# Experts of a decoder: results scattered by the names of their tokens and read back with plain loads

## The reference

```
scores = sigmoid(xt @ gate.T)
_, sel = top_k(scores + expert_bias, TOP_K)
order = argsort(sel.reshape(-1), stable=True)
token_idx = order // TOP_K;  expert_ids = sel.reshape(-1)[order]
xb = (xt[token_idx] * scores_sorted[:, None]).astype(bfloat16)
for e in range(8):
    h = silu(xb @ w1e.T) * (xb @ w3e.T)
    out_r += where(expert_ids == e, h @ w2e.T, 0)
out = (silu(xt @ shared_w1.T) * (xt @ shared_w3.T)) @ shared_w2.T
out = out.at[token_idx].add(out_r)
x = layernorm(x + out)
```

## Time and profile before

| | |
|---|---|
| median of 3 runs | 2945.8 us (2944.82 to 2948.53) |
| the profiled execution: its own time | 2947.47 us |
| its span, first to last instruction | 2945.7 us |
| mean granted TensorE clock | 0.958 |
| busy: PE, DVE, ACT, POOL | 2639.9, 1988.5, 1464.4, 1199.9 us |
| the stage `experts` begins at | about 2674 us |
| its first block begins on PE at | 2796.17 us |
| its last block's result stands in `ex_oe` at | 2871.6 us |
| its last output tile is made at | 2935.9 us |

### The profile page before, as it was taken

How to read it: one execution, slowest core, us unless ns; L and a number is a source line. 1 busy time by engine, 2 the same in 40 slices (tenths; PEclk the granted TensorE clock), 3 DMA queues, 4 the chain that set the end, 5 groups by cost and what they waited for, 6 DMA issues and landing times. The chain is left out here.

```text
span 2945.7 us, 47353 instructions
## 1 busy us (share of the span) xinstructions
PE 2639.9 (90%) x16941; PEld 1760.8 (60%) x16941; DVE 1988.5 (68%) x2542; ACT 1464.4 (50%) x2868; POOL 1199.9 (41%) x1106
## 2 busy tenths in 40 slices
PE   8999899888888888886999899999997889997886
PEld 5666645534444444443999777777775555556653
DVE  4788757689999999966112079999999733333353
ACT  3444413289999998862222166666666311112410
POOL 0000025446666565542222058688888500001304
PEclk9999999989999999997999999999999999997898
DMA  2123513269888887964002221011112271111163
GB/s 97 65 77 116 201 51 100 77 133 168 170 170 163 170 172 162 191 154 159 32 29 74 100 79 45 26 55 58 51 51 94 77 129 36 43 66 58 61 151 118
DMA packets 534873, 296.52 MB, mean 101 GB/s; under 512 B 438160, under 2 KB 482192, under 8 KB 530832
## 3 DMA queue, kind: packets, MB, share of 16 engines
q1 hardware_dynamic: 518720, 260.31, 35.1%
q0 software_dynamic: 15952, 33.56, 4.0%
HBM read 126.43 MB, written 62.78 MB: 64 GB/s over the span
## 5 line engine op out<-in xcount | busy, mean ns | idle before, releaser
L1181 DVE TENSOR_REDUCE xh_top<-xh_seen 128x1 f32<-128x512 f32 (+1 forms) x768 | 631.3, 863 | 46.0 <-PE xh_seen L1083 32.5
L1153 ACT ACTIVATE xh_prob<-xh_sc,xh_bias,xh_scale 128x1024 int16<-128x1024 f32 (+1 forms) x512 | 609.8, 1201 | 69.5 <-PE xh_sc L1083 69.3
L2328 POOL TENSOR_TENSOR ss_state<-ss_du,ss_b_all 128x1024 f32<-128x1024 f32 x128 | 445.7, 3495 | 169.4 <-PE ss_turned L1926 97.8
L1083 PE MATMUL xh_seen<-xh_kT,xh_qT 96*128 96x512 bf16 x1024 | 354.0, 387 | 81.8 <-DVE xh_top L1181 79.8
L2376 DVE TENSOR_TENSOR_SCAN ss_state<-ss_decay,ss_state 128x1024 f32<-128x1024 f32 x128 | 387.3, 3027 | 27.3 <-ACT ss_decay L2178 27.3
L1083 PE MATMUL xh_sc<-xh_kT,xh_qT 96*128 96x512 bf16 x1024 | 309.0, 384 | 1.3 <-ACT xh_prob L1153 1.3
L1207 POOL CAST xh_probT<-xh_pairs 128x2048 int16<-128x2048 uint8 x128 | 241.8, 1889 | 11.3 <-DMA xh_pairs<-xh_prob 2.7
L1083 PEld LDWEIGHTS xh_seen<-xh_kT,xh_qT 96*128 96x128 bf16 x1024 | 89.3, 97 | 242.8 <-DVE xh_top L1181 220.4
L1933 PE MATMUL ss_bank<-ss_xc,hold_w_conv 128*128 128x256 f32 x1024 | 229.3, 379 | 0.7 <-ACT ss_xc L2190 0.7
L2178 ACT ACTIVATE ss_decay<-ss_delta,ss_a 128x255 f32<-128x255 f32 x512 | 210.7, 496 | 0.4
L1933 PEld LDWEIGHTS ss_bank<-ss_xc,hold_w_conv 128*128 128x128 f32 x1024 | 190.0, 189 | 26.4 <-ACT ss_xc L2190 1.1
(11 more groups left out here) (392 smaller groups left out, 4886.5 us busy)
## 6 DMA issues: line engine op xcount, KB each, us to landing
ex_rows_in<-sa_zeros POOLq DMA_DIRECT2D x18, 1024.0 KB, 6.7
ss_b_all<-ss_states SPq DMA_DIRECT2D x8, 2048.0 KB, 7.2
xa_kT<-xp_kT SPq DMA_DIRECT2D x8, 768.0 KB, 5.3
xh_qT<-xa_qT SPq DMA_DIRECT2D x48, 128.0 KB, 3.2
xh_kT<-xa_kT SPq DMA_DIRECT2D x48, 128.0 KB, 3.3
ex_rows_out<-ex_oe SPq DMA_DIRECT2D x23, 256.0 KB, 2.2
sa_x<-in_x SPq DMA_DIRECT2D x8, 512.0 KB, 3.6
sa_y<-in_x SPq DMA_DIRECT2D x8, 512.0 KB, 10.9
```

Of the source, the lines that this page charges most:

```text
L1083: ins = pe.matmul(out[:, c * D:(c + 1) * D], qT[s][:, t * P:(t + 1) * P], kT[s][:, at + c * D:at + (c + 1) * D], start=True, stop=True)
L1153: act.activation(out, scores, ACT.Exp, bias=bias[t % RING][:, :], scale=scale[s][:, t:t + 1], accum_out=total[s][:, half, t:t + 1]).then_i ...
L1181: ins = v.tensor_reduce(top[t % RING][:, k:k + 1], scores[:, 0:n], AX.X, ALU.max)\
L2328: g.tensor_tensor(state[k % RING][:, :, :], du[s][:, :, :], spread(b_all[s][:, k, :], KD), ALU.mult)\
```

## The change

Each row that is scattered to `rows_in` gets a name, the row of a new tensor `results` in which its result belongs: 2 x token + copy. POOL scatters the names (4 bytes each) to `names_in` with four more indirect DMAs per batch. Rows that nobody fills hold a name beyond the tokens, from an iota and one DMA in the first stage. SP loads a block's 256 names behind its rows (tiles `ex_name`, four buffers), and POOL sends the block's result to the rows that the names say, with two indirect DMAs of 128 rows. SP's stores to `rows_out`, POOL's gathers and the six instructions of `plan` that made their indices are gone. At the end SP reads each batch's results with one plain load of 512 KB. The expert numbers are packed eight to a word: PE reads three words after `expand_shared(7)` and takes a block's number out of them with shifts. Two smaller edits: `count_earlier(7)` writes to a bank of `xin` and no longer waits for `placed` of batch 6, and ACT's `front(3)` stands ahead of `scale(1)`.

```diff
             def load_rows(j):
-                at = sp.value_load(table[0:1, 0, j:j + 1], min_val=0, max_val=EXPERT_ROWS - S)
+                at = sp.value_load(rows_at[0:1, j:j + 1], min_val=0, max_val=EXPERT_ROWS - S)
...
-                        sp.wait_ge(scattered[s], 16 * 2 * TB * B // 2)
+                        sp.wait_ge(scattered[s], 16 * 4 * TB * B // 2)
                 if j >= 3:
                     sp.wait_ge(up_ps, ONE + B + j - 2)
                 sp.dma_start_transpose(rowT[j % 3][:, :, :], rows_in[bass.ds(at, S), :]).then_inc(row_loaded[j % 3], 16)
-
-            for j in range(3):
+                if j >= NAMES:
+                    sp.wait_ge(oe_sent[(j - NAMES) % 3], 16 * TB * ((j - NAMES) // 3 + 1))
+                sp.dma_start(name[j % NAMES][:, :], names_in[bass.ds(at, S), :].rearrange("(t p) o -> p (t o)", p=P),
+                             allow_slow_non_contiguous=True).then_inc(name_loaded[j % NAMES], 16)
+
+            for j in range(BLOCKS):
                 load_rows(j)
-            for j in range(BLOCKS):
-                if j + 3 < BLOCKS:
-                    load_rows(j + 3)
-                sp.wait_ge(oe_ready, ONE + j + 1)
-                sp.dma_start(block_rows(rows_out, j * S), oe[j % 3][:, :, :]).then_inc(oe_stored[j % 3], 16)
+            for i in range(3):
+                sp.wait_ge(oe_sent[i], 16 * TB * ((BLOCKS - 1 - i) // 3 + 1))
+            for n in range(B):
+                if n >= PAIRS:
+                    sp.wait_ge(y_ps, ONE + n - PAIRS + 1)
+                sp.dma_start(result[n], results[n * 2 * S:(n + 1) * 2 * S, :]
+                             .rearrange("(t p c) d -> p t (c d)", p=P, c=2)).then_inc(got[n % PAIRS], 16)
             for n in range(B):
                 sp.wait_ge(y_done, ONE + n + 1)
                 sp.dma_start(tokens(x_out, n), y_out[n % 2][:, :, :]).then_inc(stored[n % 2], 16)
...
-            g.wait_ge(result_placed, ONE + 1)
-            for i in range(3):
-                g.wait_ge(oe_stored[i], ONE + 16 * ((BLOCKS - 1 - i) // 3 + 1))
-
-            def gather(n):
-                if n >= PAIRS:
-                    g.wait_ge(y_ps, ONE + n - PAIRS + 1)
                 for i in (0, 1):
                     for t in range(TB):
-                        g.indirect_dma_start(result[n][:, i, t, :], None, rows_out,
-                                             bass.IndirectOffsetOnAxis(ap=result_place[:, n, i, t:t + 1], axis=0))\
-                            .then_inc(got[n % PAIRS], 16)
-
-            gather(0)
+                        g.indirect_dma_start(names_in, bass.IndirectOffsetOnAxis(ap=place[:, n, i, t:t + 1], axis=0),
+                                             names[:, n, i, t:t + 1], None).then_inc(scattered[n % 2], 16)
+            for j in range(BLOCKS):
+                g.wait_ge(name_loaded[j % NAMES], ONE + 16 * (j // NAMES + 1))
+                g.wait_ge(oe_ready, ONE + j + 1)
+                for t in range(TB):
+                    g.indirect_dma_start(results, bass.IndirectOffsetOnAxis(ap=name[j % NAMES][:, t:t + 1], axis=0),
+                                         oe[j % 3][:, t, :], None).then_inc(oe_sent[j % 3], 16)
             for n in range(B):
-                if n + 1 < B:
-                    gather(n + 1)
                 inverse_root(g, ln, n)
...
                 pe.wait_ge(chosen, ONE + n + 1)
-                pe.wait_ge(placed, ONE + n)
+                if n < B - 1:
+                    pe.wait_ge(placed, ONE + n)
+                else:
+                    pe.wait_ge(xT_sb, ONE + B)
...
-            e = expand_shared(B - 1, between=choose_experts)
+            expand_shared(B - 1)
+            words = load_experts()
...
             front(2)
             scale(0)
             odds(2)
+            front(3)
             scale(1)
-            front(3)
             odds(3)
...
             def take(j):
                 v.wait_ge(down, ONE + j + 1)
                 if j >= 3:
-                    v.wait_ge(oe_stored[j % 3], ONE + 16 * (j // 3))
+                    v.wait_ge(oe_sent[j % 3], 16 * TB * (j // 3))
```

More of the change, by code:

```diff
@@ L2790, in experts @@
         place = p.sb("place", [P, B, 2, TB], U32)
[L2791 to L2794, removed]
+        names = p.sb("names", [P, B, 2, TB], U32)
+        name = [p.sb(f"name{i}", [P, TB], U32) for i in range(NAMES)]
         blocks = p.sb("blocks", [P, E])
@@ L2863, in _ @@
             g.memset(ln.minus_half[:, :], -0.5).then_inc(ln.half_set, 1)
+            g.iota(names[:, :, :, :].bitcast(I32), [[2 * S, B], [1, 2], [2 * P, TB]], base=0, channel_multiplier=2).then_inc(named, 1)
             g.wait_ge(ln.half_set, ONE + 1)
+            g.wait_ge(named, ONE + 1)
             for n in range(B):
@@ L2923, in count_earlier, with expand_shared, load_experts, expert @@
                 ins.then_inc(cum_ps, 1)
[L2925 to L2935 removed]
+            def expand_shared(n):
                 if n >= 2:
                     pe.wait_ge(hid_ready, ONE + n - 1)
[L2938 to L2946 removed]
+                to_features(pe, up1[n % 2], s1, 0, xT[n], KH)
+                to_features(pe, up3[n % 2], s3, 0, xT[n], KH).then_inc(up_ps, 1)
+            def load_experts():
+                pe.wait_ge(tab_ready, ONE + 1)
+                return [pe.value_load(experts_at[0:1, i:i + 1], min_val=0, max_val=E ** PER_WORD - 1) for i in range(WORDS)]
+            def expert(j):
+                return pe.snap((words[j // PER_WORD] >> (3 * (j % PER_WORD))) & (E - 1), min_val=0, max_val=E - 1)
             def expand(j, e):
@@ L2988, in add_results @@
             def add_results(n):
-                pe.wait_ge(got[n % PAIRS], 16 * 2 * TB * (n // PAIRS + 1))
+                pe.wait_ge(got[n % PAIRS], ONE + 16 * (n // PAIRS + 1))
                 for t in range(TB):
                     for i in (0, 1):
-                        ins = pe.matmul(sums[n % PAIRS][t], ident_b[:, :], result[n][:, i, t, :], start=False,
+                        ins = pe.matmul(sums[n % PAIRS][t], ident_b[:, :], result[n][:, t, i * D:(i + 1) * D], start=False,
                                         stop=(i == 1), skip_group_check=True)
@@ L3100, in _ @@
                 v.memset(numbers[:, j:j + 1], float(j))
+            v.memset(digits[:, :, :], 0.0)
+            for i in range(PER_WORD):
+                v.memset(powers[:, :, i:i + 1], float(E ** i))
             v.memset(one[:, :], 1.0)
@@ L3151, in plan @@
             def plan():
-                chain = Chain(v, chain_t, 16)
+                chain = Chain(v, chain_t, 15)
                 v.wait_ge(count_ps, ONE + 1)
@@ L3258, in decoder @@
               state_space(nc, A, after[2], after[3], hold), linear_attention(nc, A, after[3], after[4], hold),
-              experts(nc, A, after[4], out, hold.rows_in)]
+              experts(nc, A, after[4], out, hold.rows_in, hold.names_in)]
     phases = [next(stages[0])]
```

84 lines of the change are left out of this document (39 added, 45 removed).

## The result

| | before | after |
|---|---|---|
| median | 2946.91 us | 2986.53 us |
| lowest to highest | 2944.82 to 2948.53 | 2984.66 to 2990.18 |
| ratio, 95% interval | | 1.0136 (1.0119 to 1.0154) |
| span of the profiled execution | 2945.7 us | 2982.8 us |

The kernel after is slower by 1.36%, 39.6 us; forecast were 10.8 us, in a range that ended at 2967 us. To see where the time went I cut the stage at five points that every kernel has: POOL's first instruction of the stage (the memset of `ex_minus_half`), PE's first matmul on `ex_rowT`, the end of the last take, the first `ex_stats` on DVE, and the end of the last `ex_y_out`. The stages ahead differ by some us from run to run, in all kernels, and this cut leaves them out.

A forecast was written before the change was run, and what follows sets the result against it. PE's chain was taken to bound the routing, SP's order to make PE wait in the blocks, POOL to bound the end. 0.1 + 7.9 + 2.8 = +10.8 us gave 2956.6 against 2945.8 us; range 2946 to 2967.

The forecast's parts named there:

- Part A: Routing up to the first block: eight more scatters in a row on POOL; PE starts 0.1 us later.
- the slack: Routing: POOL had 7.7 us of slack while PE's chain set the pace.
- the swap: Routing: ACT's `front(3)` ahead of `scale(1)` shortens PE's wait, -2.4 us for what follows.
- Cold start: First two expands of the blocks: PE's clock is low after its long wait, +1.9 us.
- The ring: Blocks: rows wait for names, names for a scatter four blocks back; 13.8 us per four blocks, 3.50 each with 2% added.
- the clock falls in every turn: Rival, blocks: PE's idle gap lowers its clock, +0.35 us per block, +6 in all, 2962.6 us; chance 0.15.
- POOL's lag: Blocks: POOL begins an indirect DMA 0.77 us after what it waited for; 0.1 held possible.
- part B: The loop over blocks: +7.9 us, of which 1.9 is the cold start; ends +4.3 to +11.
- the ring doesn't bind: Rival, blocks: names not late, blocks at PE's 2.85 us, sum -1.8, or 2940.7 us with cheaper names; chance 0.10.
- Part C: The end: output store 0 stands behind the load of result 7, so later outputs wait; +2.8 us.
- an order that costs nothing: Rival, the end: store 0 not behind load 7, outputs at the pace of `normal`, -10.6 us; chance 0.02.
- The cover from the last take to the first norm: After the blocks: `add_shared(0)` to `(3)`, 19 us, cover the last scatter and the first four loads.

The follow-up runs named there:

- e6: The kernel after with 512 bytes scattered for each name into a tensor with rows of 512 bytes; 2972.7 us, ratio 1.0081.
- e7: The kernel after with 4 bytes scattered for each name into a tensor with rows of 512 bytes; 2979.0 us, ratio 1.0119.
- e5: The kernel after run again with nothing edited; 2986.9 us, ratio 1.0131.
- e11: As e10, but SP loads no names and POOL scatters each block to consecutive rows from a fixed table; 2932.5 us, ratio 0.9967.
- e12: As e10, names still loaded, but POOL stores each half block with a plain DMA to consecutive rows; 2934.1 us, ratio 0.9960.
- e1: The kernel after with 23 name buffers, so SP's loads of names no longer wait for a scatter's landing; 2994.6 us, ratio 1.0165.
- e9: As e1, with five `ex_oe` tiles instead of three; 2990.7 us, ratio 1.0157.
- e3: The kernel after with SP's loads of results 4 to 7 waiting for the load four before instead of PE's `add_results`; 2995.1 us, ratio 1.0165.
- e4: The kernel before with only the `front(3)` swap, `count_earlier(7)` in its own bank and packed expert numbers; 2935.0 us, ratio 0.9964.
- e8: The kernel after without scatters of names: rows of 1028 bytes in memory carry their name; 2964.5 us, ratio 1.0065.
- e10: The kernel after with the changes of e8, e1, e9 and e3 together; 2953.4 us, ratio 1.0032.
- e14: As e10, names loaded and waited for, but POOL scatters to consecutive rows from a fixed table; 2948.7 us, ratio 1.0021.
- e15: As e4, with the blocks' stores issued by POOL as plain DMAs instead of by SP; 2929.0 us, ratio 0.9943.
- e13: As e11, but the fixed table sends a block's rows to every eighth row of a region of 2048; 2948.9 us, ratio 1.0013.

## Why the prediction was wrong

The sign was right and the size a quarter. By its own steps:

- **Part A, +0.1 forecast, +14.9 measured.** The step that failed is that the names' scatter was priced by POOL's 1.27 us and given the rows' landing of 2.4. Where the names do land like rows (e6 and e7), the routing is 109.0 against 110.0 forecast (109.86 + 0.1): POOL's price, the slack and the swap were right. The packed 4-byte writes land in 7.2 us and slow the rows in the same queue to 5.4. Of the 14.8 us missing, 9.6 are the last scatter, issued 113.6 us behind POOL's first instruction instead of 104.0 since ACT and PE waited in the middle; 4.4 are its landing, and 0.8 the first rows' way to PE. I had asked what a descriptor costs its issuer, and not what it costs memory.
- **Cold start, +1.9 forecast, +2.7 measured**: the first two expands took 6.58 us against 3.90, at a clock of 0.50 in the first of them. That it starts cold was right.
- **The ring, 13.8 us per four blocks forecast, 16.1 measured.** The ring is the one described. Three terms were mis-sized: rows land and reach PE in 4.67 us instead of 3.4 (2837.21 to 2841.88), the expand behind the wait takes 3.16 instead of 2.1 because the clock falls (the rival "the clock falls in every turn" came true, 1.1 us per turn against 1.4 priced), and the scatter lands in 2.54 instead of 2.4. The take, POOL's lag (0.75) and SP's 1.26 were right. That is one turn. From the end of `expand(1)` to that of `expand(21)` five turns took 16.3, 16.1, 16.2, 15.8 and 14.4 us, 78.9 together, where the forecast had 69.1; these 9.8 us are most of the 13 missing in part B. (The same turns in e5 took 15.9, 16.2, 14.5, 14.7 and 14.8 us, so a turn is no fixed time.) The last block added 2.3 (loads of rows 4.7 us apart at the end), the cold start 0.8.
- The slow landing of rows goes with POOL's indirect DMAs (5.7 us in e11, 3.4 with plain stores in e12 on the same chip), but what in them does it was not settled. The Trainium skill (DMA: Bandwidth & Descriptors, Queues, rings and completion order) says that a DMA engine's semaphore write waits for all its earlier writes, those of other queues too; by that a row load would be reported late behind a slow scatter. The longer landing agrees; ACT's late gates, which wait for no DMA, are not explained by it.
- The rival "the ring doesn't bind" gave the blocks PE's pace. Without that wait e1 and e9 still took 90 and 82 us. Both ran on chips where ACT's gates come late, so how much of that after itself would have kept is not shown.
- **Part C, +2.8 forecast, +4.4 measured.** The mechanism is shown by e3. Store 0 took 5.2 us to its waiter instead of 3.8, and DVE waited 8.96 us for it to land. The -10.6 for an order that costs nothing was too much: e3 gives -4.9 against before.
- **Behind the last output, nothing forecast, +3.7 measured**; see the last section. The cover from the last take to the first norm held, with PE warm (-1.7).
- **The total**: 14.9 + 20.9 - 1.7 + 4.4 + 3.7 = 42.2 for the stage; e5 gives 41.3, and its medians 41.6. Two slips in the forecast's sums are too small to matter: 2874.6 less 2866.6 is 8.0 and not 7.9, and the second rival's 2940.7 counts from the profiled execution, where the median would give 2939.

## What to carry to other kernels

Price an added DMA at its landing, not at its issuer, and mistrust small scattered writes that are neighbours in memory: give each its own 512 bytes, or let a row that is written anyway carry them (routing 124.8, 109.0 and 99.4 us). Put DMAs that wait for different things into different queues; the order in SP's program was worth 9 us at the end and 8.6 us in the blocks. And undo a change part by part even when it loses: three of its edits alone gained 0.36%, and with the blocks' stores in POOL's queue 0.57%.

## What the hardware showed that I had not expected

- Neighbouring 4-byte scatters: 7.2 us median to landing in after, 2.1 us with 512 bytes between them, 2.2 us when 512 bytes were written.
- The time behind the last output goes with the number of DMAs that POOL issued in the stage, indirect or plain (e12): 64 in before and e4, 9.8 and 9.7 us; 78 in e8 and e10 to e14, 10.9 to 11.0; 87 in e15, 11.6; 110 in after, e1 to e3, e5 to e7 and e9, 13.5 to 13.6. That is about 0.08 us for each. What stands there in SP's waits, before and after (us in total, times, longest):

```profile
SPq L3273 <- PEq L3273: 5.4, 1, 5.4
```

```profile
SPq L3283 <- PEq L3283: 9.2, 1, 9.2
```

That is the barrier at the program's end; what is done for each DMA there was not tried.
- Indirect DMAs in the blocks left PE at its pace in e11 (68.9 us) and went with 82 to 90 us in e9, e10, e13, e14 and e1, with ACT's gates late by 11 to 17 us in all. Whether that is the dispersed rows, the loads of names or the chip stays open.
